# Key statistics broadcast head by head, two more groups turned by TensorE, and new orders in a two-layer cross-attention

## The chip, the cores and the metric

One core of a Trainium2 chip runs the kernel. The metric is the device time of one execution in microseconds; smaller is better. The engines are PE (TensorE), DVE (VectorE), ACT (ScalarE), POOL (GpSimd) and SP (SyncE, which here only issues transfers). They run side by side, each in its own fixed order, and wait for one another by semaphores.

## What is computed

Two cross-attentions, one after the other, for 128 independent samples of 64 queries and 64 keys, all in float32. The first has two heads with their own key input (`ctx` for head a, `fside` for head v); the second takes the result as its query:

```
def _cma(x1, x2, ...):                     # once with x2 = ctx, once with x2 = fside
    x1n = _ln(x1, ln1_g, ln1_b)
    x2n = _ln(x2, ln2_g, ln2_b)
    q, k, v = x1n @ Wq + bq, x2n @ Wk + bk, x2n @ Wv + bv
    attn = softmax(q @ k.T * scale)
    return (attn @ v) @ Wo + bo
res = out_a + out_v + text
x1  = _ln(res, ln_g, ln_b) @ fc_W + fc_b + res
# second layer: query x1 (128 wide), key and value ctx (64 wide)
Q, K, V = x1 @ Wq + bq, ctx @ Wk + bk, ctx @ Wv + bv
out = x1 + (softmax(Q @ K.T * scale) @ V) @ Wo + bo
```

## The kernel before

The 128 samples are 16 groups of 8 (`GROUPS`), a group being four pairs of samples, so that 128 partitions hold a pair. The weights are folded together once at the start (`fold_a` to `fold_t1b` on PE, small copies on DVE and ACT). For each group PE then runs `t0`, `s0` (scores of layer 0), `prob0T`, `mix0`, `out0`, `resN`, `dense`, `x1T`, `t1`, `s1` (scores of layer 1), `prob1T`, `mix1`, `out1`, with the softmax and normalisation work between them on DVE, ACT and POOL.

`t0` needs the normalised input with features on partitions (`zT_sb`), `s0` the normalised keys in the same layout (`cfT_sb`). There are two ways to these:

- A **turned** group (`TURNED = [0, 1, 2, 3]`): POOL or DVE scales the tile with samples on partitions (`z`, `scale_cf`, `shift_cf`), PE turns it (`zT`, `cfT`, four transposes each), and ACT copies it out of PSUM (`copy_zT`, `copy_cfT`).
- A **broadcast** group (4 to 15): the input is loaded already turned (`xt`, `kt`), and the statistics are brought to it. Per batch of two groups (`BATCHES`, from `SPREAD_FROM = 3` on) PE turns the 40 rows of statistics (`turn_rows`), ACT copies them (`copy_rowsT`), SP stores them to HBM (`store_rows`, 20 KB, L327) and reads them back broadcast over the partitions: `spread_x` (L334) one 512 KB transfer, `spread_k` (L343) the scales of the keys for both heads, `spread_s` (L352) their shifts, 512 KB each. POOL then does `scale_xt` (L557), `scale_kt` (L566, waits for `k_spread`) and `shift_kt` (L575, waits for `s_spread`).

The two key broadcasts have the two heads as the outermost dimension:

```
sp.dma_start(k_spread[:, at % SPREAD_SLOTS, :, :].rearrange("p g t -> p (g t)"),
             rows_dram[at, 8:24, :].rearrange("(h r) t -> h (r t)", h=2).unsqueeze(1
             ).broadcast_to([2, C, 8 * P])).then_inc(k_spread_in[at % SPREAD_SLOTS], 16)
```

Nothing plans at run time: each engine's program is a list written out by hand, group after group in a fixed interleaving (SP from L372, POOL from L590, ACT from L871, DVE from L1303, PE from L1806). All transfers but three go through SP's queue in its order; a call waits first for its slot or its data, and all that stand behind it wait too. In the ramp PE's list has `keep_busy(n, bank)`, n matmuls of a constant with a constant whose result nobody reads (18 in all, L1569).

Of the kernel before, what the change touches and what calls it, by code (L numbers as in the profile page):

```python
# [63 lines left out]
def attention_kernel(nc, x, xt, cf, kt, ct, wq, wk, wv, w128, wt, cols128, rows_dram, out):  # L64
    with ExitStack() as ctx:
# [3 lines left out]
        def sem(name):  # L69
# [48 lines left out]
        k_spread = sb("k_spread", [2 * C, SPREAD_SLOTS, 2, PAIRS * P])  # L118
        s_spread = sb("s_spread", [2 * C, SPREAD_SLOTS, 2, PAIRS * P])
# [44 lines left out]
        rows_stored, x_spread_in, k_spread_in, s_spread_in = (  # L164
            [sem(f"{n}{s}") for s in range(SPREAD_SLOTS)]
            for n in ("rows_stored", "x_spread_in", "k_spread_in", "s_spread_in"))
# [64 lines left out]

        def cf_rstd(b):

            n = len(BATCHES[b])
            return rows[:, b, 8:8 + 8 * n].rearrange("p (h g a) -> p g a h", h=2, a=PAIRS)

        def cf_shift(b):

            n = len(BATCHES[b])
            return rows[:, b, 24:24 + 8 * n].rearrange("p (h g a) -> p g a h", h=2, a=PAIRS)  # L240
# [24 lines left out]
        def spread_in(eng, sems, g):  # L265

            at = batch_of(g) - SPREAD_FROM
            eng.wait_ge(sems[at % SPREAD_SLOTS], 16 * (at // SPREAD_SLOTS + 1))
# [31 lines left out]
        def _(sp):  # L300
# [1795 lines left out]
```

## Time and profile before

| what | us |
|---|---|
| time, median of 3 runs (259.80, 262.49, 261.52) | 261.52 |
| the profiled execution, whole time | 261.23 |
| its span, first to last instruction | 259.3 |
| PE busy in the span (mean granted clock 0.809) | 161.4 |
| DVE busy | 125.2 |
| ACT busy | 114.2 |
| POOL busy | 98.4 |
| moved by DMA | 32.84 MB, mean 127 GB/s |

A profile is one execution. Busy is time in which an engine worked; what is left of the span it waited. The granted clock is the share of TensorE's full clock that the chip let through: 1.00 is 2.4 GHz, 0.50 is 1.2 GHz. A DMA share of 1 is all 16 DMA engines at work all the time.

### The profile page before, as it was taken

The numbers are of one execution on the slowest core, as the hardware profiler recorded it, in microseconds if no ns is written. First come the engines' busy times: TensorE is split into PE (matmuls) and PEld (weight loads), VectorE is DVE, ScalarE is ACT, GpSimd is POOL, SyncE is SP. The second block draws the span as 40 slices with busy tenths as digits, with TensorE's granted clock in tenths as the row PEclk, the third lists the DMA queues.
The fourth block names the chain that finished last, engine by engine and source line by source line (L and its number), as shares of the span: only waits on it lengthen the run. The fifth ranks groups of instructions, "written<-read, shape, count | busy, mean of one in ns | idle before, by whom it ended". The sixth has DMA issues, their size and how long they took to land.

```text
span 259.3 us, 6062 instructions
## 1 busy us (share of the span) xinstructions
PE 161.4 (62%) x2272; PEld 111.4 (43%) x2272; DVE 125.2 (48%) x354; ACT 114.2 (44%) x398; POOL 98.4 (38%) x121
## 2 busy tenths in 40 slices
PE   7889991382535596071999019941349151999964
PEld 7767760152313374041757016620027031676732
DVE  2899984015055279012387045913325220687773
ACT  3476782034133356030577105712408130686882
POOL 2296420713060781215840097404064124740020
PEclk9999999577558689755799858995559866899999
DMA  6999723616163071413426232724313320103014
GB/s 177 375 326 330 247 102 96 192 61 221 55 183 90 28 243 59 120 52 121 164 75 172 87 97 66 234 84 126 99 37 118 122 87 36 47 0 125 3 42 164
DMA packets 16737, 32.84 MB, mean 127 GB/s; under 512 B 1876, under 2 KB 4548, under 8 KB 16708
## 3 DMA queue, kind: packets, MB, share of 16 engines
q1 hardware_dynamic: 16276, 32.05, 37.1%
q10 hardware_dynamic: 432, 0.41, 0.6%
q8 instruction: 18, 0.29, 0.5%
q14 instruction: 11, 0.09, 0.1%
HBM read 28.13 MB, written 4.32 MB: 125 GB/s over the span
## 4 chain that ended last, share of the span: by engine, by line
DMA 45%; PE 20%; issue 18%; DVE 6%; POOL 5%; SPq 3%; ACT 2%; POOLq 0%; DVEq 0%; ACTq 0%
DMA s_spread<-rows_dram 19%; DMA rows_dram<-rowsT 14%; DMA cf_sb<-in_cf 5%; DMA k_spread<-rows_dram 2%; PE ps L1753 2%; DMA x_sb<-in_x 2%; PE ps L1694 2%; PE ps L1735 2%; DVE cf_stats L1179 2%; PE ps L1704 2%; PE ps L1768 2%; DMA out<-out_sb 2%; PE ps L1714 1%; PE ps L1803 1%; PE ps L1761 1%
## 5 line engine op out<-in xcount | busy, mean ns | idle before, releaser
L1694 PE MATMUL ps<-zT_sb,m 128*128 128x512 f32 x32 | 22.6, 794 | 33.3 <-POOL zT_sb L557 33.3
L566 POOL TENSOR_TENSOR ks_sb<-kt_sb,k_spread 128x512 f32<-128x512 f32 x12 | 15.1, 1266 | 64.2 <-DMA k_spread<-rows_dram 34.9
L575 POOL TENSOR_TENSOR cfT_sb<-ks_sb,s_spread 128x512 f32<-128x512 f32 x12 | 15.2, 1267 | 39.8 <-issue 39.7
L800 ACT ACTIVATE t_sb<-ps,m 128x512 f32<-128x512 f32 x16 | 11.0, 689 | 41.2 <-PE ps L1694 41.1
L1179 DVE BATCH_NORM_STATS2 cf_stats<-cf_sb 128x6 f32<-128x128 f32 x64 | 13.8, 280 | 27.6 <-DMA cf_sb<-in_cf 27.6
L1270 DVE SCALAR_TENSOR_TENSOR x1T_sb<-ps,row_bias,resT_sb 128x512 f32<-128x512 f32 x16 | 11.9, 744 | 29.8 <-PE ps L1761 29.5
L1704 PE MATMUL ps<-cfT_sb,t_sb 64*64 64x64 f32 x512 | 13.1, 252 | 14.6 <-issue 8.3
L1694 PEld LDWEIGHTS ps<-zT_sb,m 128*128 128x128 f32 x32 | 6.2, 235 | 36.5 <-POOL zT_sb L557 34.3
L855 ACT ACTIVATE exp<-ps,exp_bias 128x64 f32<-128x64 f32 x64 | 19.2, 318 | 2.7 <-DVE exp_bias L1287 2.7
L581 POOL TENSOR_TENSOR prob<-exp,rsum 128x512 f32<-128x512 f32 x16 | 16.8, 1047 | 7.9 <-DVE rsum L1223 7.9
L1704 PEld LDWEIGHTS ps<-cfT_sb,t_sb 64*64 64x64 f32 x512 | 11.1, 160 | 19.8 <-issue 19.3
L587 POOL TENSOR_TENSOR prob<-exp,rsum 128x256 f32<-128x256 f32 x16 | 9.8, 615 | 25.6 <-DVE rsum L1292 25.6
L1714 PE MATMUL ps<-ident,prob 128*128 128x128 f32 x64 | 11.8, 316 | 11.7 <-POOL prob L581 11.6
L836 ACT ACTIVATE gain_sb<-ps,res_rstd 128x128 f32<-128x128 f32 x64 | 18.3, 374 | 1.4 <-PE ps L1753 0.4
L1172 DVE BATCH_NORM_STATS2 x_stats<-x_sb 128x6 f32<-128x256 f32 x32 | 12.0, 416 | 14.4 <-DMA x_sb<-in_x 14.4
L1735 PE MATMUL ps<-mix_sb,w 128*128 128x512 f32 x32 | 18.6, 670 | 0.1
L1239 DVE BATCH_NORM_STATS2 res_stats<-ps 128x6 f32<-128x256 f32 x32 | 11.8, 417 | 13.9 <-PE ps L1742 13.9
L1300 DVE TENSOR_TENSOR out_sb<-ps,x1T_sb 128x512 f32<-128x512 f32 x16 | 11.0, 687 | 15.7 <-PE ps L1803 15.4
L1753 PEld LDWEIGHTS ps<-wd,resT_sb 128*128 128x128 f32 x128 | 16.9, 202 | 3.6 <-issue 3.4
L1208 DVE TENSOR_REDUCE max<-ps 128x8 f32<-128x512 f32 x16 | 10.7, 669 | 15.5 <-PE ps L1704 15.5
L1753 PE MATMUL ps<-wd,resT_sb 128*128 128x130 f32 x128 | 18.2, 289 | 0.0
L557 POOL TENSOR_TENSOR zT_sb<-xt_sb,x_spread 128x512 f32<-128x512 f32 x12 | 15.2, 1270 | 4.7 <-issue 4.7
(153 smaller groups left out, 375.0 us busy)
## 6 DMA issues: line engine op xcount, KB each, us to landing
x_sb<-in_x SPq DMA_DIRECT2D x16, 256.0 KB, 5.3
xt_sb<-in_xt SPq DMA_DIRECT2D x16, 256.0 KB, 5.4
out<-out_sb SPq DMA_DIRECT2D x16, 256.0 KB, 2.7
cf_sb<-in_cf SPq DMA_DIRECT2D x15, 256.0 KB, 6.0
kt_sb<-in_kt SPq DMA_DIRECT2D x12, 256.0 KB, 9.1
x_spread<-rows_dram SPq DMA_DIRECT2D x6, 512.0 KB, 4.7
k_spread<-rows_dram SPq DMA_DIRECT2D x6, 512.0 KB
s_spread<-rows_dram SPq DMA_DIRECT2D x6, 512.0 KB
```

Of the source, the lines that this page charges most:

```text
L557: pool.tensor_tensor(zT_sb[:, g % ZT_SLOTS, :], xt_sb[:, g % XT_SLOTS, :], x_spread[:, slot, half, :], ALU.mult).then_inc(zT_scaled, 1)
L566: pool.tensor_tensor(blocks(ks_sb[:, g % KS_SLOTS, :]), kt_sb[:, at % KT_SLOTS, :, :, :, :], blocks(k_spread[:, slot, half, :]), ALU.mult) ...
L575: pool.tensor_tensor(cfT_sb[:, g % CFT_SLOTS, :, :, :, :], blocks(ks_sb[:, g % KS_SLOTS, :]), blocks(s_spread[:, slot, half, :]), ALU.add) ...
L581: pool.tensor_tensor(prob0[:, g % PROB0_SLOTS, :, :, :], exp0[:, g % EXP0_SLOTS, :, :, :], wide0(rsum0, g), ALU.mult).then_inc(prob0_done, 1)
L836: last = nc.scalar.mul(gain_sb[:, g % GAIN_SLOTS, p, :], ps[:, bank + p // 2, at:at + D], res_rstd[:, g, p // 2, p % 2:p % 2 + 1])
L855: last = nc.scalar.activation(exp1[:, g % EXP1_SLOTS, p, :], ps[:, bank + u, v * S:(v + 1) * S], ACT.Exp, bias=exp1_bias[:, g, p:p + 1], a ...
L1179: last = v.bn_stats(cf_stats[:, g, p, :, :].rearrange("p h k -> p (h k)"), cf_sb[:, g % CF_SLOTS, p, :, :].rearrange("p h c -> p c h"))
L1694: mm(ps[:, bank, :], m0[:, 0:2 * C], zT_sb[:, g % ZT_SLOTS, :], start=True, stop=True).then_inc(t0_made, 1)
L1704: last = mm(ps[HALF[b], bank + h, p * S:(p + 1) * S], t0_sb[HALF[h], g % T0_SLOTS, p, b, :], cfT_sb[HALF[h], g % CFT_SLOTS, u, b, v, :], s ...
L1714: last = nc.tensor.transpose(ps[:, bank, at:at + P], prob0[:, g % PROB0_SLOTS, h, 2 * u:2 * u + 2, :], ident[:, :])
L1735: mm(ps[:, bank, :], w01[:, 0:D], mix0_sb[:, g % MIX0_SLOTS, :, :, :, :], start=True, stop=True).then_inc(out0_made, 1)
L1753: last = mm(ps[:, bank + p // 2, at:at + D + 2], resT_sb[:, g % REST_SLOTS, p * P:(p + 1) * P], wd[:, 0:D + 2], start=True, stop=True)
```

## The change

- `TURNED` takes in groups 4 and 5, and `SPREAD_FROM` goes from 3 to 4: five batches are broadcast, not six.
- `spread_k` and `spread_s` become one `spread_k` with one transfer per head. Each fills the 64 partitions of its head with the scales and the shifts of both groups (2048 floats). For that the 40 rows are ordered by head first (`key_rows`), and `s_spread` becomes a part of `k_spread`. `scale_kt` and `shift_kt` both wait for both transfers (32).
- All `keep_busy` calls go from PE's list.
- The lists of all five engines are new, with other PSUM banks.

```
-TURNED = [0, 1, 2, 3]
+TURNED = [0, 1, 2, 3, 4, 5]
-SPREAD_FROM = 3
+SPREAD_FROM = 4
...
-        k_spread = sb("k_spread", [2 * C, SPREAD_SLOTS, 2, PAIRS * P])
-        s_spread = sb("s_spread", [2 * C, SPREAD_SLOTS, 2, PAIRS * P])
+        k_spread = sb("k_spread", [2 * C, SPREAD_SLOTS, 2, 2, PAIRS * P])
...
+        def key_rows(b, which):
+
+            by_half = rows[:, b, 8:40].rearrange("p (h z g a) -> p z g a h", h=2, z=2, a=PAIRS)
+            return by_half[:, which, 0:len(BATCHES[b]), :, :]
+
         def cf_rstd(b):
-            n = len(BATCHES[b])
-            return rows[:, b, 8:8 + 8 * n].rearrange("p (h g a) -> p g a h", h=2, a=PAIRS)
+            return key_rows(b, 0)
...
-                    sp.wait_ge(ks_done, BATCHES[b - SPREAD_SLOTS][-1] + 1 - len(TURNED))
-                sp.dma_start(k_spread[:, at % SPREAD_SLOTS, :, :].rearrange("p g t -> p (g t)"),
-                             rows_dram[at, 8:24, :].rearrange("(h r) t -> h (r t)", h=2).unsqueeze(1
-                             ).broadcast_to([2, C, 8 * P])).then_inc(k_spread_in[at % SPREAD_SLOTS], 16)
-
-            def spread_s(b):
-                at = b - SPREAD_FROM
-                sp.wait_ge(rows_stored[at % SPREAD_SLOTS], 16 * (at // SPREAD_SLOTS + 1))
-                if at >= SPREAD_SLOTS:
                     sp.wait_ge(cfT_shifted, BATCHES[b - SPREAD_SLOTS][-1] + 1 - len(TURNED))
-                sp.dma_start(s_spread[:, at % SPREAD_SLOTS, :, :].rearrange("p g t -> p (g t)"),
-                             rows_dram[at, 24:40, :].rearrange("(h r) t -> h (r t)", h=2).unsqueeze(1
-                             ).broadcast_to([2, C, 8 * P])).then_inc(s_spread_in[at % SPREAD_SLOTS], 16)
+                for h in range(2):
+                    sp.dma_start(k_spread[HALF[h], at % SPREAD_SLOTS, :, :, :].rearrange("p z g t -> p (z g t)"),
+                                 rows_dram[at, 8 + 16 * h:24 + 16 * h, :].rearrange("r t -> (r t)").unsqueeze(0
+                                 ).broadcast_to([C, 16 * P])).then_inc(k_spread_in[at % SPREAD_SLOTS], 16)
```

SP's new list begins `load_x(0)`, `load_wv()`, `load_x(1)`, `load_wt()`, `load_wk()`, `load_w128()`, `load_cf(1)`, where before it was `load_x(0)`, `load_wk()`, `load_x(1)`, `load_wv()`, `load_x(2)`, `load_cf(1)`, `load_w128()`, `load_wt()`. PE's list, its start and the stretch from the turn of batch 5 (groups 8 and 9) to `s0(8)`:

```
             pe.wait_ge(constants_made, 1)
-            keep_busy(11, 0)
-            fold_a(0)
-            fold_v(2)
-            keep_busy(3, 7)
-            zT(0, 7)
+            fold_wv(0)
+            fold_a(6)
+            fold_v(4)
+            zT(0, 0)
...
             turn_rows(5, 3)
+            resN(4, 2)
+            mix0(5, 6, (exp1_done, 3))
+            mix1(1, 4)
+            s0(6, 2, (res_stats_done, 5), (rowsT_copied, 2))
+            x1T(3, 4, (mix1_copied, 2))
+            prob1T(2, 5)
             out0(5, 7)
+            mix1(2, 5)
+            t1(3, 4)
+            dense(4, 0, (bias_row_done, 4))
+            s1(3, 2)
+            t0(7, 4)
+            x1T(4, 7, (res_done, 6))
+            out1(1, 5)
+            s0(7, 0, (bias_row_done, 5))
+            t1(4, 7)
+            prob0T(6, 4)
+            resN(5, 2, (exp1_done, 4))
+            t0(8, 3)
+            turn_rows(6, 4, (prob0T_copied, 7))
+            mix0(6, 6, (final_done, 2))
+            s1(4, 0, (diff0_done, 8))
+            out1(2, 4, (rowsT_copied, 3))
+            t0(9, 2, (res_stats_done, 6))
+            prob1T(3, 7, (mix0_copied, 7))
+            out0(6, 6)
+            dense(5, 2, (t0_copied, 10))
+            s0(8, 4, (final_done, 3))
```

## Rows read from the trace of the kernel before

**Rows 1.** The page: busy us by engine; the chain by engine and line.

```profile
PE 161.4 (62%) x2272; PEld 111.4 (43%) x2272; DVE 125.2 (48%) x354; ACT 114.2 (44%) x398; POOL 98.4 (38%) x121
...
DMA 45%; PE 20%; issue 18%; DVE 6%; POOL 5%; SPq 3%; ACT 2%; POOLq 0%; DVEq 0%; ACTq 0%
DMA s_spread<-rows_dram 19%; DMA rows_dram<-rowsT 14%; DMA cf_sb<-in_cf 5%; DMA k_spread<-rows_dram 2%; PE ps L1753 2%; DMA x_sb<-in_x 2%; PE ps L1694 2%; PE ps L1735 2%; DVE cf_stats L1179 2%; PE ps L1704 2%; PE ps L1768 2%; DMA out<-out_sb 2%; PE ps L1714 1%; PE ps L1803 1%; PE ps L1761 1%
```

**Rows 2.** Groups by line: busy us, mean ns | idle us before, its releaser.

```profile
L557 POOL TENSOR_TENSOR zT_sb<-xt_sb,x_spread 128x512 f32<-128x512 f32 x12 | 15.2, 1270 | 4.7 <-issue 4.7
L575 POOL TENSOR_TENSOR cfT_sb<-ks_sb,s_spread 128x512 f32<-128x512 f32 x12 | 15.2, 1267 | 39.8 <-issue 39.7
L566 POOL TENSOR_TENSOR ks_sb<-kt_sb,k_spread 128x512 f32<-128x512 f32 x12 | 15.1, 1266 | 64.2 <-DMA k_spread<-rows_dram 34.9 <-issue 21.9 <-DMA x_spread<-rows_dram 7.3
...
L549 POOL TENSOR_TENSOR cfk_sb<-cfv_sb,rows 128x512 f32<-128x512 f32 x3 | 3.2, 1058 | 0.0
...
L790 ACT COPY zT_sb<-ps 128x512 f32<-128x512 f32 x4 | 2.3, 586 | 2.2 <-PE ps L1672 2.2
```

**Rows 3.** SP in order of time: start us, us taken by the issue, what.

```profile
31.20 0.59 SPq L343 DMA_DIRECT2D k_spread<-rows_dram  x1
31.83 0.51 SPq L352 DMA_DIRECT2D s_spread<-rows_dram  x1
33.86 7.98 SPq L327 DMA_DIRECT2D rows_dram<-rowsT  x1
```

**Rows 4.** POOL in order of time: start, us, what, idle before.

```profile
46.29 1.26 POOL L566 TENSOR_TENSOR ks_sb<-kt_sb,k_spread 128x512 f32<-128x512 f32 x1 [9.44 <-DMA k_spread<-rows_dram]
...
57.16 1.26 POOL L575 TENSOR_TENSOR cfT_sb<-ks_sb,s_spread 128x512 f32<-128x512 f32 x1 [5.81 <-issue]
```

**Rows 5.** The page: a kind of transfer, KB each, median us to landing.

```profile
x_spread<-rows_dram SPq DMA_DIRECT2D x6, 512.0 KB, 4.7
```

**Rows 6.** Windows: stretch, length, busy by engine, clock, DMA share, GB/s.

```profile
214.00:216.00 2.00, 0.00 (x0) 0.00 (x0) 0.00 (x0) 0.00 (x0) 0.00 (x0) 0.94 0.13 53
162.00:164.00 2.00, 1.55 (x12) 0.67 (x10) 2.00 (x6) 2.00 (x10) 0.61 (x1) 1.00 1.03 314
```

**Rows 7.** Windows of three stages: PE, PEld, DVE, ACT, POOL busy, then the clock.

```profile
7.54:40.00 32.46, 30.41 (x403) 22.43 (x402) 30.16 (x93) 23.29 (x74) 17.41 (x24) 1.00 0.78 267
40.00:222.58 182.58, 93.85 (x1298) 62.08 (x1298) 68.77 (x191) 62.27 (x217) 70.16 (x73) 0.73 0.34 111
222.58:250.00 27.42, 26.55 (x458) 18.88 (x460) 20.39 (x56) 22.09 (x83) 7.73 (x9) 1.00 0.14 51
```

**Rows 8.** The chain from 223 us: first and last of 14 operations back to back.

```profile
223.75 0.44 PE ps L1714 x4
...
231.21 0.44 PE ps L1714 x4
```

**Rows 9.** The chain: constants, then turn, copy and store of a row batch.

```profile
19.18 0.94 PE ps L1569 x6
...
158.04 0.23 PE ps L1687
158.29 0.27 ACT rowsT L785
158.58 2.33 DMA rows_dram<-rowsT
```

**Rows 10.** PE in order of time: the first constant matmuls.

```profile
1.52 5.06 PE L1569 MATMUL ps<-ones,ident 128*128 128x128 f32 x22 [1.52 <-POOL ident L500]
```

**Rows 11.** Groups by line and shape: PE's weight loads of the first two folds.

```profile
L1572 PEld LDWEIGHTS ps<-affine_a,wq_sb 128*128 128x128 f32 x2 | 0.5, 333 | 0.0
...
L1572 PEld LDWEIGHTS ps<-affine_v,wq_sb 128*128 128x128 f32 x2 | 0.3, 188 | 0.1
```

**Rows 12.** The sum over windows on the eight stretches at a clock of 0.50.

```profile
sum 99.00, PE 45.59 PEld 28.84 DVE 24.32 ACT 22.73 POOL 47.90; mean PE 5.70 PEld 3.60 DVE 3.04 ACT 2.84 POOL 5.99
```

**Rows 13.** SP's waits: waited for, us in total, times, longest.

```profile
SPq L370 <- DVE out_sb L1300: 46.4, 9, 14.8
```

More of the change, by code:

```diff
@@ L401, in _ @@
             load_xt(4)
+            load_ct(2)
+            load_x(10)
+            load_kt(6)
+            load_x(11)
             load_xt(5)
[L403 to L404 removed]
+            load_xt(6)
             load_ct(3)
[L406 to L412 removed]
+            load_ct(4)
+            load_cf(8)
+            load_x(12)
+            load_x(13)
@@ L430, in _ @@
+            load_xt(8)
+            store_rows(5)
+            load_ct(7)
+            load_xt(9)
+            load_xt(10)
+            load_cf(10)
+            spread_x(5)
+            load_cf(11)
+            spread_k(5)
+            load_kt(9)
+            load_x(15)
+            load_kt(10)
             store(0)
-            load_cf(10)
-            store_rows(5)
-            load_cf(11)
+            store_rows(6)
+            store(1)
             load_xt(11)
-            load_kt(9)
-            spread_x(5)
@@ L572, in shift_kt @@
                 pool.wait_ge(ks_done, at + 1)
-                spread_in(pool, s_spread_in, g)
+                spread_in(pool, k_spread_in, g, 32)
                 need(pool, s0_made, g - CFT_SLOTS + 1)
                 pool.tensor_tensor(cfT_sb[:, g % CFT_SLOTS, :, :, :, :], blocks(ks_sb[:, g % KS_SLOTS, :]),
-                                   blocks(s_spread[:, slot, half, :]), ALU.add).then_inc(cfT_shifted, 1)
+                                   blocks(k_spread[:, slot, 1, half, :]), ALU.add).then_inc(cfT_shifted, 1)
             def probs0(g):
@@ L648, in _ @@
+            shifts(6)
+            probs1(3)
+            scale_kt(8)
+            shift_kt(8)
+            scale_kt(9)
+            probs0(7)
+            shift_kt(9)
+            probs1(4)
+            scale_xt(10)
+            scale_cf(8)
             probs0(8)
             scale_kt(10)
+            scale_xt(11)
+            shift_kt(10)
+            probs1(5)
+            shifts(7)
             scale_kt(11)
-            probs1(5)
+            scale_cf(9)
+            probs0(9)
+            probs1(6)
@@ L987, in _ @@
[L987 to L1004 removed]
+            copy_mix0(6, 6)
@@ new lines, in _ @@
+            cfT(3, 5, (wfc_done, 1))
+            prob0T(0, 0, (t0_copied, 4))
+            zT(4, 1, (t1_bias_done, 1))
+            mix0(0, 3)
+            s0(3, 6, (diff0_done, 3))
+            zT(5, 0)
+            prob0T(1, 5)
+            out0(0, 2, (out0_bias_done, 1))
+            mix0(1, 3)
+            prob0T(2, 5)
+            resN(0, 2)
+            out0(1, 3)
+            mix0(2, 6, (diff0_done, 4))
+            dense(0, 4)
+            resN(1, 0, (zT_copied, 6))
+            out0(2, 3)
@@ new lines, in _ @@
+            dense(1, 6)
+            x1T(0, 1)
+            turn_rows(4, 0, (res_stats_done, 2))
+            t0(4, 2)
+            cfT(4, 3, (res_done, 3))
+            resN(2, 5, (bias_row_done, 1))
+            x1T(1, 0, (rowsT_copied, 1))
+            t1(0, 1)
+            t0(5, 2, (t0_copied, 5))
+            prob0T(3, 1, (t1_copied, 1))
+            cfT(5, 3)
+            s1(0, 6, (bias_row_done, 2))
+            s0(4, 4)
+            mix0(3, 0, (x1T_done, 2))
+            s0(5, 2)
+            t1(1, 0, (mix0_copied, 4))
@@ new lines, in _ @@
+            x1T(6, 7)
+            t0(10, 6)
+            mix0(8, 0, (res_done, 8))
+            out1(4, 4)
+            t1(6, 7)
+            resN(7, 2, (exp1_done, 6))
+            s0(10, 0, (mix0_copied, 9))
+            s1(6, 6)
+            prob1T(5, 5, (final_done, 5))
+            turn_rows(7, 4)
+            t0(11, 2, (res_stats_done, 8))
+            out0(8, 3)
+            dense(7, 4, (prob1T_copied, 6))
+            mix1(5, 6, (exp1_done, 7))
+            resN(8, 0)
+            prob1T(6, 1)
@@ new lines, in _ @@
+            t1(8, 2)
+            out1(6, 6, (exp1_done, 8))
+            mix0(10, 3)
+            dense(9, 0, (res_stats_done, 10), (t0_copied, 13))
+            turn_rows(8, 2)
+            s1(8, 3, (mix0_copied, 11))
+            s0(12, 5, (final_done, 7))
+            out0(10, 2, (rowsT_copied, 5))
+            t0(13, 7)
+            x1T(9, 0, (bias_row_done, 10))
+            prob0T(11, 6, (diff0_done, 13))
+            resN(10, 1)
+            prob1T(7, 2)
+            t1(9, 0)
+            mix0(11, 5)
```

1268 lines of the change are left out of this document (568 added, 700 removed).

## Prediction

> **What bounds the kernel now.** I read the page first. No engine is full: PE is busy for 62% of the span, DVE for 48%, ACT for 44%, POOL for 38%, while the chain that ended last is DMA for 45% of its length, 19% on `s_spread` and 14% on `rows_dram` [rows 1]. So the kernel waits for transfers, above all for the broadcasts of the statistics.
>
> Next the groups of POOL, the engine that consumes the broadcasts. `ks_sb` (L566) has 64.2 us of idle time ahead of it, `cfT_sb` (L575) 39.8 and `zT_sb` (L557) 4.7: 108.7 us in all [rows 2]. Much of it carries the releaser "issue", so the order of time has to settle what it is. For the first broadcast batch (groups 4 and 5) `k_spread` is issued at 31.20 and `s_spread` at 31.83 [rows 3]; the multiply with `k_spread` starts at 46.29 and the add with `s_spread` at 57.16, each behind a wait [rows 4]. A pair of key broadcasts (1 MB) takes some 25 us from issue to use, where `x_spread`, with 512 KB as large as each of the two, lands in a median of 4.7 us [rows 5].
>
> The windows say why. Where almost nothing but a key broadcast is under way, the 16 DMA engines are busy for 0.13 of the time and move 53 GB/s: 0.13 x 16 = 2.1 engines at some 25 GB/s each. With all of them at work the same queue moves 314 GB/s at a share of 1.03 [rows 6]. The key broadcast has a destination of [2, C, 8 x 128], so 2 is its outermost size; that of `x_spread` is [128, 1024]. At 53 GB/s, 1 MB takes 20 us. Whatever has a part on those two engines queues up behind it: issuing the row store at 33.86 alone took 7.98 us [rows 3].
>
> Last, the stages. From 7.54 to 40 us the kernel is dense (PE busy 30.41 of 32.46 us, DVE 30.16), and from 222.58 to 250 again (PE 26.55 of 27.42). Between 40 and 222.58 us PE is busy for 93.85 of 182.58 us and the granted clock is 0.73 [rows 7]. In that middle stage the broadcasts are waited for, and there the change can pay.
>
> **Key broadcasts, one transfer per head.** `spread_k` now issues two transfers of [64, 2048] f32, 512 KB each, in place of two of [2, 64, 1024]; bytes and number of issues stay. No row of before shows a large broadcast of this shape. The nearest by shape is `x_spread`, with a large outermost size too, which lands in 4.7 us [rows 5]; the other bound is a transfer that stays on two engines, 10 us for 512 KB at 53 GB/s [rows 6]. I take the former: 4.7 us for `x_spread`, and 1 MB / 314 GB/s = 3.3 us behind it for both heads, so that the pair lands some 8 us after the issue of `x_spread`, not 25.
>
> The Trainium skill has a rule for this ("DMA: Bandwidth & Descriptors", section "Why a DMA increments its semaphore by 16 and not by 1"): a transfer uses the largest number of engines up to 16 that divides the outermost size of both sides. By it a size of 2 gives two engines, with which the share of 0.13 agrees, and 64 would give 16, which no row here shows for a large transfer. Another rule of the Trainium skill speaks against the new form: "SBUF — State Buffer", section "Door 1: The DMA port swizzle (why `[64,N]` ≈ `[32,N]`)", says that a tile on 64 partitions reaches half of the ports that one on 128 reaches. By it the pair would take 6.6 us in place of 3.3 and the sum would come out as in the first rival; no row here shows it.
>
> Does work cover the new latency? In the new order of PE 18 operations stand between `turn_rows(5)` and `t0(8)`, the tightest of the five batches. At full clock 14 operations of the same kinds ran back to back from 223.75 to 231.65, 0.56 us each [rows 8]: 10.2 us of cover. The need is 0.5 for the turn and its copy, 2.33 for the store [rows 9], 4.7 for `x_spread` and 1.27 for `scale_xt` [rows 2, 5]: 8.8 us. Up to `s0(8)` nine more operations add 5.1 us (15.3), and the need grows by 3.3 + 2 x 1.27 to 14.6. So the route is just covered and nothing of the 108.7 us need stay. One new wait is free: `spread_k` waits for `cfT_shifted` of two batches back, not `ks_done`, one add of 1.27 us later and long past.
>
> **Six turned groups.** Groups 4 and 5 leave the broadcast route. POOL loses six instructions of 1.27 us and gets four of 1.06 (`z`, `shift_cf`) [rows 2]: -3.4 us. PE gets 16 transposes, 4 of which take 0.44 us [rows 8]: +1.8. ACT gets four copies of 0.59 us [rows 2]: +2.3. The DMA loses 1.5 MB of broadcasts and 0.5 MB of `kt`. All this lies in the ramp and the middle stage and is counted in the latter.
>
> **Ramp.** 18 constant matmuls go. The first 11 calls (22 instructions, 5.06 us from 1.52 on) filled a time in which nothing was loaded [rows 10]; three of the others stood on the chain at 19.18 with 0.94 us [rows 9]. PE now starts with `fold_wv`, which needs `wv` and POOL's products; `wk`, which the next two folds need, is fifth on SP, not second, and an issue there takes some 0.5 us [rows 3], so it comes perhaps 1 us later. The clock is the larger matter. The weight loads of the first fold on `affine_a` took 333 ns each, those on `affine_v` a microsecond later 188 [rows 11]: PE began at its lower level (1.2 of 2.4 GHz), though the profile reads a granted clock of 1.00 there, and rose only about 7 us, after 5 us of constants. Without them its first real work runs at half speed. PE and DVE are busy alike in this stage (30.4 and 30.2 us [rows 7]), so a PE slowed over some 5 us of work loses up to 5 us. Bounds: -2.4 (the later seven calls and nothing lost) and +5; I take +2, since DVE and the loads cover part of it.
>
> **The sum**, against the span of 259.3 us. Ramp and first groups, to 40 us: 40 + 2 = 42. End, from 222.58 on, where no broadcast is waited for: 36.7, kept. Middle: PE is busy 93.85 us, 45.59 of them in the 99.0 us at half clock, which all lie here [rows 12]; at full clock that is 93.85 - 45.59 / 2 = 71.1, with the transposes 73. DVE has 68.8 us there, POOL 70.2 - 3.4 = 66.8, ACT 62.3 + 2.3 = 64.6 [rows 7]. Four engines with nearly equal loads in fixed orders don't pack: the dense stretches reached 94 and 97% of PE, but with POOL at 54 and 28%. I take 82%: 73 / 0.82 = 89. Sum 42 + 89 + 36.7 = 167.7; the run took 261.23 us around its span of 259.3, so +1.9: **169.5 us**. The profiled run lies 0.3 us under the median of 261.52, which is nothing here. The forecast's own range: 95% of PE gives 77, and with -2.4 in the ramp 153; 73% gives 100, and with +5 in the ramp 184.
>
> **Rivals.**
> 1. *Ports.* A transfer to 64 partitions moves at half the rate, the pair takes 6.6 us. The need for `s0(8)` becomes 17.9 us against 15.3 of cover; about 2 us stay per batch, x 5 = +10: 180 us. For it: no row shows a large 64-partition transfer at full rate. Against it: the two heads follow each other in one queue and may overlap. (It is the rule of the Trainium skill's SBUF page.)
> 2. *The route is the wait.* SP is one queue, and it spent 46.4 us waiting for outputs to store [rows 13]; a row store or a broadcast behind such a wait is late whatever its speed. If each batch stays 7 us late, x 5 = +35: 205 us. For it: the cover is just enough. Against it: those waits were themselves made by late groups.
> 3. *It does not spread.* The new transfers stay on two engines, 1 MB keeps its 20 us, and only the first batch is saved, whose waits were 9.4 + 5.8 = 15 us [rows 4]: 261.5 - 15 + 2 = 248 us. `x_spread` speaks against it.
> 4. *Slower.* A transfer that reads one source row goes to one engine: 512 KB at 25 GB/s takes 20 us, the pair 41, 21 more than now, x 5 = +105, less the 15 of the first batch, +2 for the ramp: 353 us. It decides from 23 us per pair on (5 x 3 us against 13). `x_spread` also reads one row for all partitions and lands in 4.7 us, which speaks against it.
>
> **How the numbers follow.** Forecast 0.60, ports 0.20, route 0.14, no spreading 0.04, one engine 0.02. The range must hold 0.8: from 153, the forecast's lower end, to 190, past the ports' case; the other three are left out. A difference under about 1% of 261.5 us can't be told from none. Faster by over 1% is all but the last, less a remainder: 0.97; within 1% 0.01; slower 0.02.
>
> **What the profile after would show.** The broadcast spreads: no stretch with a share near 0.13 at 50 GB/s, and issues on SP back at 0.5 us. The waits go: idle time ahead of L557, L566 and L575 from 108.7 to under 20 us. The middle: PE over 80% busy at a granted clock over 0.9. The ramp: its first matmuls at half speed, and the first groups some 2 us later. I am wrong if the middle stays over 110 us long; then the row store or SP is late (rival 2), or DVE, POOL or ACT, loaded alike, wait for each other in the new orders.

## The result, and the profile after

The changed kernel takes a third less time. Changed kernel: 175.03 us median of 4 runs (174.70 to 175.83). Kernel before beside it: 261.15 us (259.80 to 262.49). Ratio 0.671, interval 0.666 to 0.675. The forecast was 169.5 us with a range of 153 to 190.

Run again on another occasion, the unchanged file of the changed kernel gave 177.26 us (6 runs, 173.33 to 179.89). The runs of this kernel and of its variants spread over 1 to 9 us, those of the kernel before over 3 to 7 us; differences of 2 us between variants are not read here. The ratios are formed from undisturbed (fast) runs alone, so they need not be the quotient of two medians.

The page of the profiled execution of the changed kernel: busy time by engine; PE by 40 equal slices, the granted clock, the share of the DMA engines; then the chain that ended last.

```profile
PE 147.0 (85%) x2251; PEld 101.6 (59%) x2251; DVE 127.9 (74%) x354; ACT 112.6 (65%) x401; POOL 95.2 (55%) x119
...
PE   0599999999997999796719989949996989999872
...
PEclk9999999999999999999996999996999999999998
DMA  5996091796999169999977059963991101400114
...
PE 54%; DVE 11%; DMA 11%; issue 11%; ACT 6%; POOL 3%; SPq 2%; DVEq 0%; POOLq 0%; ACTq 0%
```

PE is busy for 85% of a span of 173.6 us, where it was busy for 62% of 259.3 [rows 1]. The chain is work of PE for 54%, where it was DMA for 45%. The granted clock is full in nearly every slice. The kernel has changed its bound.

The groups of POOL that consume the broadcasts, the matmuls of `t0` behind them, and the two kinds of broadcast with their time to landing:

```profile
L549 POOL TENSOR_TENSOR ks_sb<-kt_sb,k_spread 128x512 f32<-128x512 f32 x10 | 12.7, 1269 | 7.2 <-DMA k_spread<-rows_dram 5.6
L540 POOL TENSOR_TENSOR zT_sb<-xt_sb,x_spread 128x512 f32<-128x512 f32 x10 | 12.6, 1271 | 6.5 <-DMA x_spread<-rows_dram 3.1
L558 POOL TENSOR_TENSOR cfT_sb<-ks_sb,k_spread 128x512 f32<-128x512 f32 x10 | 12.7, 1274 | 0.4
...
L1678 PE MATMUL ps<-zT_sb,m 128*128 128x512 f32 x32 | 18.6, 678 | 0.4 <-POOL zT_sb L540 0.4
...
k_spread<-rows_dram SPq DMA_DIRECT2D x10, 512.0 KB, 8.1
...
x_spread<-rows_dram SPq DMA_DIRECT2D x5, 512.0 KB, 6.0
```

The idle time ahead of POOL's three is 7.2 + 6.5 + 0.4 = 14.1 us; it was 108.7 [rows 2]. PE itself now waits for `zT_sb` for 0.4 us in all.

The windows cut the span at 44 us, at the one long stop of PE, and behind the last shift of the keys at 138.67. By DVE's busy time the first and the last boundary stand for the same work as 40 and 222.58 us in the kernel before, to within some 1 us: 31.8 us of DVE ahead of the first there and 32.2 in before, 23.4 and 24.2 us behind the last.

```profile
0.00:44.00 44.00, 37.42 (x393) 27.94 (x393) 31.80 (x104) 25.78 (x74) 23.52 (x43) 1.00 0.68 225
...
44.00:85.82 41.82, 37.51 (x687) 25.33 (x686) 36.67 (x97) 30.90 (x112) 27.56 (x30) 1.00 0.86 231
85.82:90.31 4.49, 0.00 (x0) 0.00 (x0) 0.00 (x0) 0.00 (x0) 2.92 (x4) 1.00 0.91 244
90.31:138.67 48.36, 43.14 (x677) 29.01 (x676) 36.00 (x93) 32.05 (x118) 32.48 (x35) 0.93 0.60 161
...
138.67:173.60 34.93, 28.91 (x508) 19.29 (x500) 23.39 (x62) 23.90 (x99) 8.76 (x12) 0.98 0.18 66
```

The middle stage takes 94.7 us (182.6 before [rows 7]). On either side of the stop PE is busy for 90% and 89% of it. In the stop itself DVE and ACT do nothing either: they are waiting for PE. PE in order of time names nothing that PE waited for:

```profile
84.31 1.13 PE L1737 MATMUL ps<-wd,resT_sb 128*128 128x130 f32 x8
85.37 0.45 PE L1779 MATMUL ps<-prob1T_sb,cf_sb 64*64 64x64 f32 x13
90.31 0.33 PE L1779 MATMUL ps<-prob1T_sb,cf_sb 64*64 64x64 f32 x3 [4.49 <-issue]
```

It stops after 13 of the 16 matmuls of one operation, whose operands are all there.

### The profile page after: what moved, and what is told of

The parts are those of the page before. It is cut to its first block, busy times and chain, and to the rows that moved or that the text cites. A ratio compares the mean times of both kernels' runs of the same rounds, so it can differ in the third digit from the quotient of the medians.

```text
span 173.6 us, 6018 instructions
## 1 busy us (share of the span) xinstructions
PE 147.0 (85%) x2251; PEld 101.6 (59%) x2251; DVE 127.9 (74%) x354; ACT 112.6 (65%) x401; POOL 95.2 (55%) x119
## 4 chain that ended last, share of the span: by engine, by line
PE 54%; DVE 11%; DMA 11%; issue 11%; ACT 6%; POOL 3%; SPq 2%; DVEq 0%; POOLq 0%; ACTq 0%
PE ps L1719 7%; PE ps L1737 6%; DMA cf_sb<-in_cf 6%; PE ps L1678 5%; ACT exp L836 4%; DMA k_spread<-rows_dram 4%; PE ps L1752 4%; PE ps L1688 4%; PE ps L1710 3%; PE ps L1726 3%; PE ps L1745 3%; PE ps L1779 3%; PE ps L1656 2%; PE ps L1698 2%; PE ps L1787 2%
## 5 line engine op out<-in xcount | busy, mean ns | idle before, releaser
L1678 PE MATMUL ps<-zT_sb,m 128*128 128x512 f32 x32 | 18.6, 678 | 0.4 <-POOL zT_sb L540 0.4
L549 POOL TENSOR_TENSOR ks_sb<-kt_sb,k_spread 128x512 f32<-128x512 f32 x10 | 12.7, 1269 | 7.2 <-DMA k_spread<-rows_dram 5.6
L540 POOL TENSOR_TENSOR zT_sb<-xt_sb,x_spread 128x512 f32<-128x512 f32 x10 | 12.6, 1271 | 6.5 <-DMA x_spread<-rows_dram 3.1
L525 POOL TENSOR_TENSOR cfv_sb<-cf_sb,rows 128x512 f32<-128x512 f32 x15 | 15.9, 1058 | 0.1
L1217 DVE SCALAR_TENSOR_TENSOR resT_sb<-ps,out_bias,xt_sb 128x512 f32<-128x512 f32 x16 | 11.9, 743 | 3.3 <-PE ps L1719 3.2
L800 ACT COPY prob0T_sb<-ps 128x512 f32<-128x512 f32 x16 | 9.5, 595 | 6.8 <-PE ps L1698 6.7
L836 ACT ACTIVATION_READ_ACCUMULATOR exp<-ps,exp_bias 128x1 f32 x64 | 13.7, 214 | 0.0
L1259 DVE TENSOR_REDUCE minus_max<-ps 128x4 f32<-128x256 f32 x16 | 6.7, 419 | 9.4 <-PE ps L1762 9.3
L1779 PE MATMUL ps<-prob1T_sb,cf_sb 64*64 64x64 f32 x256 | 7.4, 227 | 6.7 <-issue 4.5
L558 POOL TENSOR_TENSOR cfT_sb<-ks_sb,k_spread 128x512 f32<-128x512 f32 x10 | 12.7, 1274 | 0.4
```

What stands on the lines that cost most here:

```text
L525: pool.tensor_tensor(cfv_sb[:, g % CFV_SLOTS, :, :, :], cf_sb[:, g % CF_SLOTS, :, :, :], wide_cf(cf_rstd, g), ALU.mult).then_inc(cfv_pool, 1)
L549: pool.tensor_tensor(blocks(ks_sb[:, g % KS_SLOTS, :]), kt_sb[:, at % KT_SLOTS, :, :, :, :], blocks(k_spread[:, slot, 0, half, :]), ALU.mu ...
L558: pool.tensor_tensor(cfT_sb[:, g % CFT_SLOTS, :, :, :, :], blocks(ks_sb[:, g % KS_SLOTS, :]), blocks(k_spread[:, slot, 1, half, :]), ALU.a ...
L836: last = nc.scalar.activation(exp1[:, g % EXP1_SLOTS, p, :], ps[:, bank + u, v * S:(v + 1) * S], ACT.Exp, bias=exp1_bias[:, g, p:p + 1], a ...
L1678: mm(ps[:, bank, :], m0[:, 0:2 * C], zT_sb[:, g % ZT_SLOTS, :], start=True, stop=True).then_inc(t0_made, 1)
L1779: last = mm(ps[HALF[u], bank + v, b * S:(b + 1) * S], cf_sb[HALF[v], g % CF_SLOTS, 2 * u + b, 0, :], prob1T_sb[HALF[v], g % PROB1T_SLOTS, ...
```

## What the experiments asked

Three things were open: whether the shape of the broadcast is really the whole gain (against the new orders and the two turned groups); whether a broadcast to 64 partitions runs at half rate, as the first rival had it, and what that costs here; and where the 5.5 us above the forecast lie: the ramp without constants, or the stop at 85.82 us.

### The shape alone, undone and done

First, the changed kernel with the old shape of destination:

```diff
-                for h in range(2):
-                    sp.dma_start(k_spread[HALF[h], at % SPREAD_SLOTS, :, :, :].rearrange("p z g t -> p (z g t)"),
-                                 rows_dram[at, 8 + 16 * h:24 + 16 * h, :].rearrange("r t -> (r t)").unsqueeze(0
-                                 ).broadcast_to([C, 16 * P])).then_inc(k_spread_in[at % SPREAD_SLOTS], 16)
+                for z in range(2):
+                    sp.dma_start(k_spread[:, at % SPREAD_SLOTS, z, :, :].rearrange("p g t -> p (g t)"),
+                                 rows_dram[at, 8:40, :].rearrange("(h z r) t -> z h (r t)", h=2, z=2)[z].unsqueeze(1
+                                 ).broadcast_to([2, C, 8 * P])).then_inc(k_spread_in[at % SPREAD_SLOTS], 16)
```

> The changed kernel with its new lists and six turned groups, but the key broadcasts again as two transfers of [2, 64, 1024] (scales of both heads, shifts of both heads). Theory 'shape': the broadcasts' two engines are the whole story, so the pair takes 20 us again where 15 us of work cover it, some 15 us are lost per batch, x 5 = +75: 240 to 260 us, with windows at a DMA share of 0.13. Rival 'lists and turned groups': they carry a good part of the gain, and the time stays under 210 us.

Measured: 255.04 us (253.47 to 256.69), ratio 0.980 (0.971 to 0.989). Its windows (length, PE, PEld, DVE, ACT, POOL busy, clock, DMA share, GB/s) and its group of `ks_sb`:

```profile
70.00:80.00 10.00, 5.08 (x94) 4.13 (x95) 5.70 (x16) 3.87 (x19) 4.91 (x7) 0.58 0.13 42
...
L549 POOL TENSOR_TENSOR ks_sb<-kt_sb,k_spread 128x512 f32<-128x512 f32 x10 | 12.6, 1265 | 86.7 <-DMA k_spread<-rows_dram 69.3
```

The share of 0.13 is back, with 86.7 us of idle time ahead of `ks_sb`. All other parts of the change together are worth 2% while the old shape stands.

Second, the kernel before with its own lists, its four turned groups and its constants, and nothing but the new `spread_k` (with one tile and one count of arrivals for both statistics, which it needs; both transfers of a batch are issued where the first of the two stood):

```diff
             spread_k(4)
...
-            spread_s(4)
```

> The kernel before with only the key broadcasts changed: one transfer per head and the rows ordered by head, both issued where the first of the two broadcasts stood; four turned groups, constants and all lists as before. Theory 'shape': almost all of the gain comes, 175 to 190 us, a little more than the changed kernel for a sixth batch. Rival 'lists and turned groups': without them the row route is not covered and the time stays over 205 us.

Measured: 180.78 us (176.98 to 182.84), ratio 0.686 (0.676 to 0.696). Of some 86 us, about 80 come from the shape; orders, turned groups and constants together add some 3.5 to 6 (180.78 against 177.26 and 175.03); how these divide was not tried. The theory that the lists carry a good part of the gain is out, and so are rivals 3 and 4 of the prediction (it does not spread; one row makes one engine).

The Trainium skill's rule in "DMA: Bandwidth & Descriptors", section "Why a DMA increments its semaphore by 16 and not by 1", gives 2 engines for an outermost size of 2 and 16 for one of 64. Both runs agree: a share of 0.13 with the one, of 0.97 to 1.05 with the other in the transfers timed alone (below).

### What a transfer to 64 partitions moves

> Leaves out the whole computation and stores part of the broadcasts as output: only transfers, one stage after the other. Theory 'ports': 512 KB to 64 partitions alone takes longer than 512 KB to 128 partitions (about 3.3 us and more of moving time against 1.6), three of them to the same half move at about 160 GB/s, while low and high half in turn recover part of it. Rival 'no port limit': all forms but [2, 64, 1024] move at 300 GB/s or more. The two-head form moves at 50 GB/s and 0.13 in both.

Measured, in windows of a run that computes nothing (length, POOL busy, clock, DMA share, GB/s): 512 KB to all 128 partitions, to the lower half, to the upper half, and to the halves in turn.

```profile
20.00:23.00 3.00, 0.00 (x0) 1.00 0.92 354
28.00:31.00 3.00, 0.00 (x0) 1.00 1.01 208
38.00:40.00 2.00, 0.00 (x0) 1.00 0.97 197
44.00:53.00 9.00, 0.00 (x0) 1.00 0.99 218
```

All 16 DMA engines are busy in each, but to 64 partitions they move 197 to 208 GB/s, not 354: 0.56 to 0.59 of it. Two halves one behind the other hardly overlap: 218 GB/s. The windows leave out the start of each stage. In its first full microsecond a 64-partition stage still moved 303 to 352 GB/s (35 to 36 and 45 to 46 us of the run with six kinds of transfer, below), so one short transfer alone loses less than the steady rate says. The old form, with the two heads outermost, moved 52 GB/s at a share of 0.13 (70 to 80 us), as both theories had it.

The Trainium skill says in "SBUF — State Buffer", section "Door 1: The DMA port swizzle (why `[64,N]` ≈ `[32,N]`)", that 64 partitions reach half of the ports, and in the section "Can I just issue two DMAs to hit both halves?" that two transfers to the two halves, measured at once, gained 6% over one. These windows agree with the direction of the first (somewhat more than half) and with the second: 218 is 5 to 11% over 197 to 208.

What it costs this kernel was measured with the same megabyte sent as two transfers of [128, 1024], for which every partition gets the rows of head a:

```diff
-                for h in range(2):
...
+                for z in range(2):
+                    sp.dma_start(k_spread[:, at % SPREAD_SLOTS, z, :, :].rearrange("p g t -> p (g t)"),
+                                 rows_dram[at, 8 + 8 * z:16 + 8 * z, :].rearrange("r t -> (r t)").unsqueeze(0
+                                 ).broadcast_to([P, 8 * P])).then_inc(k_spread_in[at % SPREAD_SLOTS], 16)
```

> The changed kernel with the same 1 MB per batch sent as two transfers to all 128 partitions, so that head v gets rows of head a for its keys: the statistics of half the keys are the wrong ones, the amount of work is the same. Theory 'ports': the pair lands 1.5 to 3 us sooner and DMA is less crowded, 170 to 173 us. Rival 'cover': the work hides the difference, 174 to 176 us.

Measured: 168.40 us (165.84 to 169.75), ratio 0.641 (0.635 to 0.648). The page: the key broadcasts and the wait for them.

```profile
L549 POOL TENSOR_TENSOR ks_sb<-kt_sb,k_spread 128x512 f32<-128x512 f32 x10 | 12.7, 1269 | 1.6 <-DMA k_spread<-rows_dram 1.6
...
k_spread<-rows_dram SPq DMA_DIRECT2D x10, 512.0 KB, 6.3
```

It is 6.6 us under 175.03 and 8.9 under the second measurement of the changed kernel, more than the theory expected. A broadcast lands in 6.3 us, not 8.1; 5.6 us of waiting ahead of `ks_sb` go, and the stop inside an operation shrinks from 4.49 to 1.44 us (below), which is 3.05 of the 5.9 us between the two profiled executions. The lower rate of 64 partitions costs this kernel some 7 us.

### Can all partitions be had with the right rows?

Two more stores of 64 KB put eight copies of each head's rows into memory, and each broadcast then reads 16 source rows for 8 partitions each:

```diff
+                for h in range(2):
+                    sp.dma_start(key_copies[at, h, :, :, :].rearrange("q r t -> r q t"),
+                                 rowsT[8 + 16 * h:24 + 16 * h, at % SPREAD_SLOTS, :].unsqueeze(1).broadcast_to([16, 8, P])
+                                 ).then_inc(keys_stored[at % SPREAD_SLOTS], 16)
...
+                for z in range(2):
+                    sp.dma_start(k_spread[:, at % SPREAD_SLOTS, z, :, :].rearrange("p g t -> p (g t)"),
+                                 key_copies[at, :, :, 8 * z:8 * z + 8, :].rearrange("h q r t -> (h q) (r t)").unsqueeze(1
+                                 ).broadcast_to([16, 8, 8 * P])).then_inc(k_spread_in[at % SPREAD_SLOTS], 16)
```

> The changed kernel with all its values, in which the key statistics reach all 128 partitions in one transfer over all engines: beside the row store, two more stores put eight copies of each head's 16 rows into memory (64 KB each, in pieces of 512 bytes), and each of the two broadcasts is then [16, 8, 1024], 16 source rows for 8 partitions each, in place of [64, 2048] for one half. Theory one (a transfer to 64 partitions runs at 205 to 250 GB/s, one to 128 at 350, and this costs the changed kernel the 6.6 us that the run with full width and wrong statistics gained): the pair lands about 1.5 us earlier, the copies cost 1 to 2 us of latency behind the row store, and the time is 169 to 173 us. Rival: the copies of 512 bytes and the two more issues on SP take back what the width gives, or a source with 16 rows runs no faster than 250 GB/s; then it is 175 to 179 us, as the changed kernel itself.

Measured: 177.65 us (175.44 to 181.03), ratio 0.678 (0.672 to 0.684): no gain. A broadcast lands in a median of 8.0 us (8.1 in the changed kernel), so the new form is no faster. Six kinds of transfer, each alone, say why:

> None of the attention is computed: six kinds of transfer of 512 KB are timed, three at once of each, alone on the chip, in this order: one row to 128 partitions; 16 rows to 8 partitions each; 128 rows, one for each of 128 partitions; one row to 64 partitions; 64 rows, one for each of 64 partitions; 64 rows to 2 partitions each. The question is why the run with copied rows moved its statistics no faster than the changed kernel. Theory one: the number of partitions written is what counts. Then the first, second, third and sixth kinds move 330 to 380 GB/s and the fourth and fifth 200 to 250, and the copied rows were slow only because of other transfers beside them. Rival: what counts is which partitions each of the 16 engines is given. Transfer kinds in which an engine has a few neighbouring partitions to itself (the second, the sixth) stay at 200 to 250 GB/s although 128 partitions are written, and the one-row kind alone, or it and the plain load, reach 330 to 380.

Measured, in windows as above: one row to 128 partitions; 16 rows to 8 partitions each; 128 rows to 128; one row to 64; 64 rows to 64; 64 rows to 2 partitions each.

```profile
12.00:15.00 3.00, 0.00 (x0) 1.00 0.95 337
20.00:23.00 3.00, 0.00 (x0) 1.00 1.03 235
28.00:31.00 3.00, 0.00 (x0) 1.00 0.98 325
36.00:40.00 4.00, 0.00 (x0) 1.00 1.05 213
46.00:50.00 4.00, 0.00 (x0) 1.00 0.99 203
55.00:58.00 3.00, 0.00 (x0) 1.00 0.93 284
```

Neither theory holds alone. With 64 partitions it is 203 to 213 GB/s, from one row or from 64 (the first theory). But 16 rows to 8 partitions each reach only 235, though all 128 partitions are written (the rival), and 64 rows to 2 each 284. So the grouping of partitions counts as well as their number. How the partitions fall to the 16 engines in each form was not seen, and is left open.

### The constants and the ramp

Three runs put constants back or took them out. Into the changed kernel went 14 of them as below, and in the next run 9: 7 ahead of `fold_wv`, 2 behind it, none ahead of `zT(0)`.

```diff
+            keep_busy(8, 3)
...
+            keep_busy(3, 3)
...
+            keep_busy(3, 3)
```

> The changed kernel with 14 constant matmuls put back at the start of PE's list (8 before fold_wv, 3 after it, 3 before zT(0)). Theory 'clock': the first scores s0(0), at 22.17 us in the changed kernel and 16.44 in the one before, come at about 17 to 18 us, and the time falls by 3 to 5 us to some 171 us. Rival 'new ramp order': the folds stand ahead of the first groups and loads come later, so the constants only add their own time: s0(0) stays after 20 us and the time at 174 to 177 us.

> The changed kernel with nine constant matmuls put back, 7 before fold_wv and 2 in the gap behind it, in time that PE idled; none before zT(0). Theory 'clock': the upper level comes before 16 us, s0(0) at 18 to 20 us in place of 22.2, and the time is 172 to 173.5 us. Rival 'the ramp is not what decides': s0(0) comes earlier, but the median stays within 1.5 us of 175, because later stalls take it back.

Measured: with 14, 177.70 us (172.61 to 181.09), ratio 0.665 (0.658 to 0.673), which can't be told from the 0.671 of the changed kernel; with 9, 180.40 us (177.96 to 182.62), ratio 0.690 (0.684 to 0.697), slower than it. And the kernel with the new shape alone, without its constants:

```diff
-            keep_busy(11, 0)
             fold_a(0)
             fold_v(2)
-            keep_busy(3, 7)
...
-            keep_busy(3, 1, (diff0_done, 1))
-            s0(1, 1)
+            s0(1, 1, (diff0_done, 1))
```

> The lists of the kernel before with the new broadcasts (as in e2_shape_alone), and all 18 constant matmuls taken out; the two waits that constants carried go to the s0 behind them. Theory 'clock': PE starts cold, the first scores come some 3 us later than with constants and the time rises from 181 to 183 to 186 us. Rival: the constants bought nothing here, 178 to 182 us.

Measured: 182.39 us (181.69 to 185.06), ratio 0.701 (0.697 to 0.706), against 180.78 and 0.686 with them: 1.6 us between the medians, some 4 us by the ratios (0.015 of 261 us), whose intervals are just apart (0.696 and 0.697). That the constants are worth something there is likely, as the theory of the clock has it; how much is not firm, by the spread of these runs.

In the changed kernel's ramp the matmuls of L1678 show the clock. PE in order of time (start, us, what):

```profile
19.48 2.77 PE L1678 MATMUL ps<-zT_sb,m 128*128 128x512 f32 x3
22.17 0.74 PE L1688 MATMUL ps<-cfT_sb,t_sb 64*64 64x64 f32 x32
...
24.61 1.02 PE L1678 MATMUL ps<-zT_sb,m 128*128 128x512 f32 x2
```

0.92 us each up to 22 us, 0.51 each after: by these durations PE runs at its lower level (1.2 of 2.4 GHz) until then, although it is busy for 10.00 of the 10 us from 10 to 20 and the profile reads a granted clock of 1.00 there. The first scores, `s0(0)`, start at 22.17; with 9 constants at 21.53, with 14 at 19.62, in the kernel before at 16.44. So 14 constants do win 2.5 us in the ramp, 9 win 0.6; for 14 neither expectation held, since `s0(0)` came between the two. In the profiled executions both gains are lost again further on, and with 9 more than that: this run was slower than both expectations had it. Two of the six runs with 14 took 172.61 and 172.92 us, under all ten of the changed kernel (173.33 at least); no trace of these two was kept, so whether 14 constants sometimes keep their gain is open. PE of the profiled run with 14 constants:

```profile
48.81 0.44 PE L1779 MATMUL ps<-prob1T_sb,cf_sb 64*64 64x64 f32 x10
53.09 0.49 PE L1779 MATMUL ps<-prob1T_sb,cf_sb 64*64 64x64 f32 x6 [3.84 <-issue]
```

Another stop in the middle of one operation, with nothing to wait for that the profile shows.

### The stops inside an operation

The page lists a DMA queue that carries instructions, 18 transfers of 16 KB:

```profile
q8 instruction: 18, 0.29, 0.7%
```

PE and its sequencer have 4658 instructions on record, the four other engines 1,360 together. In the trace I counted the instructions of PE and its sequencer that had started at each stop, and looked up the 16 KB transfer nearest to it (us):

| kernel | instructions before the stop | block transfer starts, takes | PE goes on | stop |
|---|---|---|---|---|
| changed | 2241 | 87.9, 1.18 | 90.31 | 4.49 |
| changed, run again | 2241 | 87.7, 1.21 | 90.30 | 4.93 |
| later loads (below) | 2241 | 87.4, 1.47 | 90.31 | 5.21 |
| copied rows | 2241 | 89.4, 1.40 | 92.18 | 4.39 |
| full width | 2241 | 85.1, 1.04 | 87.46 | 1.44 |
| 14 constants | 1217 | 50.1, 1.39 | 53.09 | 3.84 |
| 9 constants | 1217 | 51.4, 1.37 | 54.38 | 3.10 |

The kernel with the new shape alone has such stops too, at 1217, 1729 and 3009, of 1.73, 2.32 and 1.25 us; without its constants it stops at 1985 and 3265, for 0.96 and 1.96 us; and the kernel with 14 constants stops again at 2241, for 1.17 us. Programs with other operations at that place stop at the same counts, and all six counts lie whole multiples of 256 apart (1985 and 2241 by one); 4658 / 256 = 18.2 then gives the 18 transfers. So these are PE's program, in blocks of 256 instructions. In each row PE goes on 1.2 to 1.6 us after the end of the block's transfer. PE stops because its next instructions have not arrived. At 1217 the changed kernel stops too, for 0.9 us, and the two with constants for 3.84 and 3.10: they get there at 49.25 and 51.28 us, not at 53.54, but go on at 53.09 and 54.38, not much before the 54.47 of the changed kernel. At the same place of the program the run with 14 was 2.1 us ahead of the changed kernel just before its stop (49.03 against 51.10 us) and 2.0 us behind it just after (53.09 against 51.11). The time won in the ramp ends at this block.

Why the block is late: the changed kernel passes instruction 1985 at 80.02 us, and the transfer of the block that it needs at 2241 starts 7.9 us later. In the last quarter, with a DMA share of 0.18, the transfers start 0.6, 1.0 and 1.3 us after it has passed 3777, 4033 and 4545 (at 4289 it starts 0.2 us ahead, so the count is good to a few instructions only). The stop at 85.82 falls in a stretch with a DMA share of 0.91, behind a broadcast pair issued from 78.44 on and five loads. If the loads were to blame, moving them would help:

```diff
-            load_ct(9)
-            load_ct(10)
-            load_xt(13)
...
+            load_ct(9)
+            load_xt(13)
+            load_ct(10)
```

> The changed kernel with the loads ct(9), ct(10) and xt(13), which nothing reads before 100 us, moved on SP behind kt(12), out of the crowded stretch from 75 to 90 us. In that stretch PE stopped for 4.49 us in the middle of a mix1, while a block of its own instructions was being read. Theory 'instruction block late behind data': the stop at 85.8 us shrinks to under 2 us and the time falls to 171 to 173.5 us. Rival: the stop has another cause and stays, 174.5 to 176 us.

Measured: 178.27 us (two runs of 174.4, four of 178.2 to 178.9). Against 175.03 and 177.26 for the changed kernel it is no gain, and the stop is there, at the same instruction:

```profile
84.65 0.45 PE L1779 MATMUL ps<-prob1T_sb,cf_sb 64*64 64x64 f32 x13
90.31 0.37 PE L1779 MATMUL ps<-prob1T_sb,cf_sb 64*64 64x64 f32 x2 [5.21 <-issue]
```

So it is not those three loads that hold the block up. What shortens the stop is a faster pair: 1.44 us with full width, at the same instruction, where the transfer starts 4.9 us after 1985 and not 7.9.

> The changed kernel once more, without an edit, so that the variants tried before have it on their own footing. Where the stop of 4.5 us inside the mixing of values is a matter of the program and not of the moment, it comes again at the same instruction, and the time is 174 to 177 us. If it is a matter of the moment, it comes elsewhere or not, and times spread from 170 to 180 us.

Measured: 177.26 us (173.33 to 179.89), the kernel before beside it 262.10 (259.09 to 263.58). The stop is at the same instruction, so it belongs to the program; the time still spreads over 6 us, so both halves of the expectation were right in part.

> None of the attention is computed: this run only prices two things. TensorE multiplies a tile of zeros by one of zeros 990 times with nothing to wait for, in three stretches of 330: with no transfer under way, with key broadcasts to 64 partitions under way without a break (three of 512 KB outstanding), and with broadcasts to 128 partitions under way (three of 512 KB). Theory one: the stop of 4.49 us in the changed kernel is a 16 KB block of TensorE's instructions that waits behind data in the transfer queues. Then the first stretch has no stop over 0.5 us, and the second has one of 1 to 5 us about every 256 instructions, 4 or 5 of them; the third has fewer or shorter ones. Rival: instructions come ahead of need whatever is under way, no stretch has a stop over 0.5 us, and the stop in the changed kernel has another cause. After that, 4 MB go to the two halves of the partitions at once, one half from SP's queue and one from ScalarE's, and then 4 MB from SP's queue in 256 KB pieces that change halves each time. If the halves use different ports, the two queues reach 320 to 350 GB/s together (12 to 13 us for 4 MB); if something else limits a 64-partition transfer, they stay at 205 to 240 (17 to 20 us). Pieces in one queue: 230 to 250 GB/s, as for whole halves in turn.

Measured: the first theory's stops did not appear in any stretch, as the rival had it. The likely reason, which I had not seen, is that PE ran so slowly here that 256 instructions last 27.4 us, and a late block still comes in time. But the lateness itself can be read. With nothing else under way, a block's transfer starts when PE is 153 to 160 instructions past a multiple of 256 (9 of 9; counted from its first record, which need not be where a block begins). Behind the 64-partition broadcasts it starts at 198, 182 and 188; behind the 128-partition ones at 181, 178 and 178. At 0.107 us per instruction, that is 3.0 to 4.7 us and some 2.6 to 2.9 us late. The windows of the stretches (length, PE, PEld, POOL busy, clock, share, GB/s):

```profile
0.00:143.00 143.00, 142.01 (x666) 142.01 (x666) 0.41 (x5) 1.00 0.00 1
145.00:225.00 80.00, 80.00 (x377) 80.00 (x377) 0.00 (x0) 1.00 0.94 192
...
285.00:370.00 85.00, 85.00 (x400) 85.00 (x400) 0.00 (x0) 1.00 0.95 293
...
432.00:440.00 8.00, 0.00 (x0) 0.00 (x0) 0.00 (x0) 1.00 1.01 250
448.00:460.00 12.00, 0.00 (x0) 0.00 (x0) 0.00 (x0) 1.00 1.04 234
```

So blocks do queue behind data, by 3 to 5 us with 1.5 MB under way; in the attention kernel PE takes only 5 to 12 us for 256 instructions, and the 7.9 us above were enough to stop it. The last two windows price the other question: the two halves from two queues at once reach 250 GB/s, over the 205 to 240 of the one expectation and far under the 320 to 350 of the other; pieces in turn in one queue reach 234. Against 197 to 208 for one half, 250 is 20 to 27% more. No ordering of 64-partition transfers came near 350.

The Trainium skill, "Runtime: NRT & Kernel Launch", section "Instruction fetch mechanics", says that instructions come in blocks of 16 KiB, 256 instructions, and that crossing a boundary is mostly hidden. The block size agrees with the count of 256. "Mostly hidden" holds by number, since 16 of the 18 boundaries of the changed kernel show no stop of over 0.7 us; it does not hold for the time, since beside broadcasts one boundary costs 4.4 to 5.2 us, in four runs of three programs.

## Why the prediction came out as it did

What decides the time was forecast rightly: the broadcasts spread, their waits go, PE becomes the bound. The rate of a 64-partition transfer, the length of the slow ramp and PE's load in the middle were not. The time lies 5.5 us over the central value, within the range. By the terms of the sum:

- **What bounds it, and the spreading.** Right. Undone alone, it gives 255 us; done alone, 181.
- **The waits.** Forecast: none of the 108.7 us need stay, under 20 to be seen. 14.1 stay. The cover was cut too fine: I gave `x_spread` 4.7 us and the pair 3.3 us more, at 314 GB/s. `x_spread` now takes 6.0, and the pair moves at some 205 to 250 GB/s, 4.2 to 5.1 us. Here the first rival was nearer, though its 6.6 us for the pair was too long: it took half of 314 GB/s, and measured was 0.56 to 0.59 of 354, and more at the start of a transfer. Batch 5 was not the tightest for `s0` either: in PE's list 23 operations stand between `turn_rows(8)` and `s0(14)`, 13.0 us of cover at 0.56 us each for the 14.6 us that I needed; `ks_sb` waits for 1.92 us there.
- **Ramp, +2.** It was +4: 44 us where the kernel before is at 40. The step was to take the lower level as lasting some 5 us of work; it lasted until 22.3 us. The bound of +5 held.
- **Middle, 73 us of PE at 82% = 89.** It took 94.7, by three errors. PE's work was 80.65 us, not 73: partly because the lower level does not double a duration. The weight loads of [rows 11] have 333 / 188 = 1.77, by which the 45.59 us of [rows 12] shrink by 19.8, not 22.8 us: +3.0, which I could have read there. Another 1.5 us is the 3.40 us at half clock behind the stop. The rest, some 3 us, is mostly the boundary: 508 matmuls lie behind it where 548 did in the kernel before, and PE has 28.9 us of work there, not 31.2, so that 2.3 us of the end are counted in the middle. The packing was better than I took, 90%, not 82%: 80.65 / 0.895 = 90.1. And the stop of 4.49 us, which no row of before foretold, comes on top: 94.6.
- **End, kept at 36.7.** 34.9, since some of its work lies ahead of the boundary.

44 + 94.7 + 34.9 + 1.8 around the span = 175.4, the profiled run. So the central value was near partly by luck: too little work for PE and too loose a packing offset each other, and the ramp's 2 us and the stop's 4.5 us are what is left.

**The rivals.** *Ports*: the lower rate of a 64-partition transfer is real, and was priced at +10 us; the run with full width puts it at about 7, by a faster pair and by a shorter stop of PE, which the rival did not have. It was wrong to set it against the forecast as an alternative, since it acts together with it: the truth, 175, lies between 169.5 and 180. *The route and SP*: not so. SP still waits for outputs to store, but the POOL groups wait 14.1 us in all, not 35. *Doesn't spread* and *slower*: excluded by the two runs on the shape.

**What the profile was to show.** No stretch at a share of 0.13 with a broadcast under way: right (behind 138.67 us the share is 0.18, with stores of outputs alone for the most part). Issues on SP back at 0.5 us: right for `k_spread` (0.59 median, 1.03 at most). Waits under 20 us: 14.1. Middle over 80% busy: 85% with the stop, at a granted clock of 0.93 to 1.00. Ramp at half speed, first groups 2 us later: at half speed, but `s0(0)` came 5.7 us and `s0(1)` 5.9 us later, not 2.

No version with the right values was found that beats the changed kernel by more than its spread.

## What to carry to other kernels

Before touching an order, read the share of the DMA engines while one transfer is alone: 0.13 is two of 16 engines, and here an outermost size of 2 in the access pattern made it so; that one line was worth 80 of 86 us. A share of 1.0 is not yet full rate: see that the GB/s beside it match those of a transfer to all 128 partitions. When an engine stops inside one operation with "issue" as the reason, count its instructions up to there, in two builds: if the counts differ by multiples of 256 or not at all, it is most likely waiting for its own program behind your data, and an edit that adds or takes instructions ahead of it moves the stop elsewhere, so that small variants can't be compared by their total time alone.

## What was not expected of the hardware

- The transfer of a block of TensorE's instructions starts 3.0 to 4.7 us late behind three broadcasts of 512 KB to 64 partitions, 2.6 to 2.9 us late behind such to 128. In the kernel such a late block stopped TensorE for 4.4 to 5.2 us behind instruction 2241, in four runs of three programs.
- With all 16 DMA engines busy, 512 KB transfers one behind the other move 197 to 213 GB/s to 64 partitions, 235 when 16 rows go to 8 partitions each, 284 when 64 rows go to 2 each, and 325 to 354 to 128. Two queues at once for the two halves: 250.
- In the run without transfers to wait for, TensorE multiplied tiles of zeros for 422 us, busy for 89% of the span, and its weight loads took 333 ns (median and longest of 1980; the shortest 286), the duration of the lower level in [rows 11], while the profile reads a granted clock of 1.00. Which products lift it from there was not tried:

```profile
L127 PE MATMUL ps<-ones 128*128 128x64 f32 x1980 | 422.7, 421 | 1.0 <-POOL ones L70 1.0
L127 PEld LDWEIGHTS ps<-ones 128*128 128x128 f32 x1980 | 422.5, 333 | 1.0 <-POOL ones L70 1.0
```
